# Far scores for two units at once from 64 contraction rows, in an attention, scan and feed-forward block on one core

## The reference

```
Q, K, V = x @ Wq.T, x @ Wk.T, x @ Wv.T          # 16 heads of 8
scores  = Q K^T * 8 ** -0.5
mask    = causal & ((col >= row - 31) | ((row - col) % 64 == 0))
attn    = softmax(where(mask, scores, -inf));    x += (attn @ V) @ Wo.T
h = s0 * [x, -x] @ sign(k0); relu * 2; s1 * h @ sign(k1); relu * 2; s2 * h @ sign(k2)   # feed-forward, added to x
state-space block: layernorm, conv over 4 steps, silu, dt = softplus(...),
  h = exp(dt * A) * h + dt * u * B ;  y = sum over 16 states of C * h     # 256 channels, a scan over time
feed-forward again
```

## Time and profile before

| | |
|---|---|
| median of 3 runs | 812.72 us |
| the profiled execution | 811.52 us, span of the core 809.7 us |
| PE busy | 721.4 us (89%) |
| DVE busy | 695.3 us (86%) |
| POOL busy | 664.2 us (82%) |
| ACT busy | 594.8 us (73%) |
| mean granted PE clock | 0.989 |

### The profile page before, as it was taken

One profiled execution on the slowest core, in us unless ns is written; L12 is line 12 of the kernel. 1 busy time (PEld: TensorE's weight loads), 2 busy tenths in 40 slices (PEclk: granted clock), 3 DMA queues, 4 the chain that ended last, 5 costly groups with the idle time before them and its releaser, 6 DMA issues. The chain is left out here.

```text
span 809.7 us, 22189 instructions
## 1 busy us (share of the span) xinstructions
PE 721.4 (89%) x7840; PEld 430.6 (53%) x7840; DVE 695.3 (86%) x1187; ACT 594.8 (73%) x1161; POOL 664.2 (82%) x824
## 2 busy tenths in 40 slices
PE   5999988998789999998999999899896889897887
PEld 3765655644455447545555456355452356453566
DVE  6977229999999989999889999999998989799983
ACT  5776698797788989887689978868667744764533
POOL 5143437998899989989999799899998999999961
PEclk9999999999999999999999999999999999998999
DMA  5000019888799668877777889889797899898950
GB/s 200 3 3 2 2 54 269 226 231 229 206 225 237 159 173 238 230 177 200 198 213 197 225 233 243 232 230 244 207 253 199 252 259 240 215 266 235 264 158 27
DMA packets 84177, 154.94 MB, mean 191 GB/s; under 512 B 9433, under 2 KB 10082, under 8 KB 84066
## 3 DMA queue, kind: packets, MB, share of 16 engines
q1 hardware_dynamic: 84066, 153.51, 71.4%
HBM read 142.46 MB, written 11.01 MB: 190 GB/s over the span
## 5 line engine op out<-in xcount | busy, mean ns | idle before, releaser
L1779 POOL TENSOR_TENSOR d<-d,cr 128x1024 f32<-128x1024 f32 x128 | 300.0, 2354 | 13.8 <-DVE d L1279 4.1
L1578 ACT ACTIVATE ps<-dt,An 128x512 f32<-128x512 f32 x256 | 173.7, 690 | 71.9 <-DVE d L1279 60.5
L1279 DVE TENSOR_TENSOR_SCAN d<-ps,hl,d 128x512 f32<-128x512 f32 x128 | 157.0, 1262 | 3.7 <-ACT ps L1578 3.3
L1279 DVE TENSOR_TENSOR_SCAN d<-ps,d 128x512 f32<-128x512 f32 x128 | 149.6, 1202 | 7.2 <-ACT ps L1578 6.5
L1267 DVE TENSOR_TENSOR d<-ps,d 128x512 f32<-128x512 f32 x184 | 118.5, 671 | 7.1 <-DMA d<-dud 7.1
L891 PE MATMUL ps<-h,w 128*128 128x512 f16 (+1 forms) x512 | 114.3, 373 | 3.5 <-DVE h L1224 2.8
L1766 POOL TENSOR_TENSOR d<-d,br 128x512 f32<-128x512 f32 x72 | 91.5, 1277 | 4.3 <-DMA d<-dud 4.3
L891 PEld LDWEIGHTS ps<-h,w 128*128 128x128 f16 x512 | 46.8, 98 | 70.9 <-DVE h L1224 12.8
L966 PE MATMUL ps<-d,cst 128*32 128x512 f32 x512 | 69.3, 614 | 10.6 <-POOL d L1779 6.4
L1434 ACT COPY pt<-ps 128x512 f32<-128x512 f32 x96 | 53.8, 589 | 13.9 <-PE ps L825 10.6
L825 PE MATMUL ps<-cst,sx 128*128 128x128 f32 x384 | 56.3, 281 | 8.0 <-ACT sx L1427 3.5
(11 more groups left out here) (182 smaller groups left out, 1457.1 us busy)
## 6 DMA issues: line engine op xcount, KB each, us to landing
dt<-dtd SPq DMA_DIRECT2D x256, 256.0 KB, 5.3
d<-dud SPq DMA_DIRECT2D x256, 256.0 KB, 4.8
dtd<-sR SPq DMA_DIRECT2D x16, 256.0 KB, 4.4
dud<-sE SPq DMA_DIRECT2D x16, 256.0 KB, 3.8
X<-in_x SPq DMA_DIRECT2D x8, 256.0 KB, 6.3
br<-bcd SPq DMA_DIRECT2D x8, 256.0 KB
cr<-bcd SPq DMA_DIRECT2D x8, 256.0 KB
out<-X SPq DMA_DIRECT2D x3, 512.0 KB, 5.8
```

Source lines behind the costliest of these rows:

```text
L1279: eng.tensor_tensor_scan(d, banks[u % NG][:, :], d, hl[:, r:r + 1] if m % 2 else 0.0, ALU.mult, ALU.add).then_inc(v_sc, 1)
L1578: eng.activation(banks[u % NG][:, :], DT[:, u % NT, :], ACT.Exp, scale=An[:, g:g + 1]).then_inc(s_da, 1)
L1779: eng.tensor_tensor(d, d, CR[m % 2][:, :].unsqueeze(1).to_broadcast((128, n, 512)), ALU.mult).then_inc(p_cm, n)
```

## The change

A far unit now has the eight heads of one half of the contraction rows and eight windows (before: all heads and four windows), and far units are made in pairs like near ones. The number of units is the same. Per far pair PE issues two mask products of 64 rows each (rows 0 to 63 and 64 to 127, in two banks) and 16 products of 64 contraction rows by 128 output rows by 64 columns. Per near pair it issues two such mask products and 8 products of 64 by 128 by 128 columns, in place of two full mask products and 16 of 64 by 64 by 128. `KD` has two copies instead of four, made by full 128 x 512 instructions scaled by a new constant `rmask` of ones and zeros per partition. POOL zeroes only the 64 leading columns of `KD`. The product with V keeps 16 products of 36 columns for a far unit. The second unit's flag (`t_sc`) comes with the pair's last product in both kinds.

All of `PLACES` is new. By its numbers, the median distance from the issue of a `du` row to its drive goes from 8351 to 9365, and from the issue of a `dt` row to its decay from 9727 to 10818. `WARM` goes from 28 entries with 152 products to 38 entries with 244 products; before the first scan there are five entries (18 products) where there were none.

```diff
-for _name, _n in (("ident", 128), ("qmask", 4), ("csel", 56), ("one8", 1)):
+for _name, _n in (("ident", 128), ("qmask", 4), ("csel", 56), ("one8", 1), ("rmask", 2)):
...
+    put("rmask", (p[:, None] // 32 % 2 == np.arange(2)[None, :]).astype(np.float32))
...
-UNITS = [(kind, g, kk) for kind, g in GROUPS for kk in range(2 if kind else 4)]
+UNITS = [(kind, g, kk, c) for kind, g in GROUPS for kk in range(1 if kind else 2) for c in range(2)]
...
 WARM = [
-    (125411, 2, 3), (127268, 2, 3), (173374, 5, 2), (180024, 6, 3), (216097, 5, 3), (460277, 5, 4), (465961, 2, 2), (505221, 7, 5),
...
+    (103369, 5, 4), (109970, 7, 5), (112856, 2, 3), (117704, 2, 2), (124035, 2, 4), (127533, 2, 7), (156348, 5, 3), (171612, 4, 3),
...
-        KD = sb("KD", [128, 4, PAD + T])
+        KD = sb("KD", [128, 2, PAD + T])
...
-        ZF = [sb(f"zf{i}", [128, 4, 4, 16]) for i in range(3)]
+        ZF = [sb(f"zf{i}", [128, 8, 2, 16]) for i in range(3)]
...
             def asc_t(b, u):
...
+                half = [slice(64 * c, 64 * c + 64) for c in range(2)]
+                two = []
+                for c in range(2):
+                    by = (s_exp, U + c + 1) if u + c in SHIFTED_T else (v_sub, shifted(b, u + c, "v") + 1)
+                    bank = bank_of["sc", b, u + c] = turn(by)
+                    if kind:
+                        mk = masks[half[c], 256:288].unsqueeze(1).to_broadcast((64, 16, 32))
...
+                    eng.matmul(bank[:, :], e4[half[c], :], mk, start=True, stop=False, skip_group_check=True)
+                    two.append(bank[:, :].rearrange("p (a w k) -> p a w k", a=2, w=nw))
...
-                    for k in range(4):
-                        m = 8 * g + 4 * kk + k
-                        lq = qm[:, 4 * kk + k, :, :].rearrange("p a n -> p (a n)")
-                        t = eng.matmul(bw[:, :, k, :].rearrange("p a (h x) -> p a h x", x=4), lq, Ks[:, :, :, 4 * m:4 * m + 4], start=False,
-                                       stop=(k == 3 and u not in SHIFTED_T), skip_group_check=True)
-                    t.then_inc(t_sc, 1)
-                    return
...
+                for k in range(nw):
+                    wi = nw * kk + k
+                    m = 8 * g + wi
                     for c in range(2):
...
+                        lq = qm[half[c], wi, :, :].rearrange("p a n -> p (a n)")
+                        dst = two[c][:, :, k, :]
+                        if kind:
+                            rk, dst = Ks[half[c], :, :, 4 * m:4 * m + 4], dst.rearrange("p a (h x) -> p a h x", x=4)
+                        else:
+                            at = 64 * (m % 16) + m // 16
+                            rk = KD[half[c], :, at:at + 127:2]
+                        t = eng.matmul(dst, lq, rk, start=False, stop=(k == nw - 1 and u + c not in SHIFTED_T), skip_group_check=True)
+                        if k == nw - 1:
                             t.then_inc(t_sc, 1)
...
-                eng.tensor_copy(e4[:, 32 * k:32 * k + 32], ident[:, 0:32]).then_inc(v_set, 2 if k == 3 else 1)
+                eng.tensor_tensor(e4[:, 32 * k:32 * k + 32], ident[:, 0:32], ident[:, 64:96], ALU.add).then_inc(v_set, 2 if k == 3 else 1)
...
-                    eng.wait_ge(p_set, 3)
                     eng.wait_ge(t_aqk, 1)
-                    for a in range(4):
-                        t = eng.tensor_copy(KD[32 * a:32 * a + 32, a, PAD:PAD + T:2], bank_of["aqk", b, 0, 1][32 * a:32 * a + 32, :])
+                    for a in range(2):
+                        t = eng.tensor_scalar(KD[:, a, PAD:PAD + T:2], bank_of["aqk", b, 0, 1][:, :], rmask[:, a:a + 1], None, ALU.mult)
...
-                for a in range(4):
-                    t = eng.copy(KD[32 * a:32 * a + 32, a, PAD + h:PAD + T:2], bank_of["aqk", b, h, 1][32 * a:32 * a + 32, :])
+                for a in range(2):
+                    t = eng.activation(KD[:, a, PAD + h:PAD + T:2], bank_of["aqk", b, h, 1][:, :], ACT.Identity, scale=rmask[:, a:a + 1])
...
-            eng.memset(KD[:, 0:3, :], 0.0).then_inc(p_set, 1)
+            eng.memset(KD[:, :, 0:PAD], 0.0).then_inc(p_set, 1)
...
-                eng.memset(KD[:, 3:4, :], 0.0).then_inc(p_set, 1)
```

More of the change, by code:

```diff
@@ L151 @@
     (UNITS_OF, 'aown_s apv_t asc_s asc_v atr_s atr_t'),
[L152 removed]
+    ([(b, u) for b, u in UNITS_OF if u % 2 == 0], 'asc_t'),
     ([(b, u) for b, u in UNITS_OF if u in SHIFTED_T], 'asb_t'),
@@ L748, in aval_t @@
                 t.then_inc(t_av, 1)
-            def scores(b, u, mk):
-                U = NU * b + u
-                bank = bank_of["sc", b, u] = turn((s_exp, U + 1) if u in SHIFTED_T else (v_sub, shifted(b, u, "v") + 1))
-                eng.matmul(bank[:, :], e4[:, :], mk, start=True, stop=False, skip_group_check=True)
-                return bank
             def asc_t(b, u):
-                kind, g, kk = UNITS[u]
+                kind, g, kk, _ = UNITS[u]
                 U, gi = NU * b + u, group_of(u)
+                nw = 8 if kind else 4
                 if U == 0:
                     eng.wait_ge(v_set, V_SEL)
-                if kind:
-                    bank = scores(b, u, masks[:, 256:288].unsqueeze(1).to_broadcast((128, 16, 32)))
-                else:
-                    kk, _ = near(u)
-                    if g == kk == 0:
-                        mk = masks[:, 0:256].unsqueeze(1).to_broadcast((128, 2, 256))
-                    else:
-                        mk = masks[:, 64:192].unsqueeze(1).to_broadcast((128, 4, 128))
-                    two = [scores(b, u + c, mk) for c in range(2)]
+                half = [slice(64 * c, 64 * c + 64) for c in range(2)]
[5 more added lines that the diff above has]
+                        mk = masks[half[c], 256:288].unsqueeze(1).to_broadcast((64, 16, 32))
+                    elif g == kk == 0:
+                        mk = masks[half[c], 0:256].unsqueeze(1).to_broadcast((64, 2, 256))
+                    else:
+                        mk = masks[half[c], 64:192].unsqueeze(1).to_broadcast((64, 4, 128))
+                    eng.matmul(bank[:, :], e4[half[c], :], mk, start=True, stop=False, skip_group_check=True)
+                    two.append(bank[:, :].rearrange("p (a w k) -> p a w k", a=2, w=nw))
                 if b == 0:
@@ L789, in asc_t @@
-                if g == 2:
-                    eng.wait_ge(p_kp, b + 1)
-                for k in range(4):
-                    m = 8 * g + 4 * kk + k
-                    at = 64 * (m % 16) + m // 16
-                    for c in range(2):
-                        r = slice(64 * c, 64 * c + 64)
-                        for j in range(2):
-                            o = slice(64 * j, 64 * j + 64)
-                            lq = qm[r, 4 * kk + k, 2 * j:2 * j + 2, :].rearrange("p a n -> p (a n)")
-                            dst = two[c][o, :].rearrange("p (a w k) -> p a w k", a=2, w=4)[:, :, k, :]
-                            t = eng.matmul(dst, lq, KD[r, 2 * c:2 * c + 2, at:at + 127:2], start=False,
-                                           stop=(k == 3 and u + c not in SHIFTED_T), skip_group_check=True)
-                        if k == 3:
+                Ks = KD[:, :, PAD:PAD + T].rearrange("p a (h x) -> p a h x", x=128)
@@ L1143, in asc_v @@
                 else:
-                    kk, c = near(u)
                     mm = MN[g % 2][:, 4 * kk:4 * kk + 4, 2 * c:2 * c + 2].rearrange("p w a -> p a w")
@@ L1361, in aqk_s @@
                         return
-                    eng.wait_ge(p_set, 3)
-                    for a in range(4):
-                        t = eng.copy(KD[32 * a:32 * a + 32, a, PAD + 1:PAD + T:2], bank_of["aqk", b, 1, 1][32 * a:32 * a + 32, :])
+                    for a in range(2):
+                        t = eng.activation(KD[:, a, PAD + 1:PAD + T:2], bank_of["aqk", b, 1, 1][:, :], ACT.Identity, scale=rmask[:, a:a + 1])
                     t.then_inc(s_aqk, 1)
```

276 lines of the change are left out of this document (136 added, 140 removed), and 318 rows, old and new, of tables (PLACES, WARM).

## The result

The changed kernel takes **823.21 us** (median of 10 runs, 817.05 to 831.07) against 812.98 us (808.44 to 818.95) for the kernel before on the same chip: a ratio of **1.0111, interval 1.0068 to 1.0154**. The ratio is that of the means without one execution of the changed kernel in which the chip was in a slower state (831.07 us), so it isn't the quotient of the two medians. By the medians the kernel is 10 us slower, by the ratio 9, where 6.5 us faster was forecast; the number lies in the range that was given, in the corner of rival B (822 us).

The account below looks back on a forecast made before the run. PE was taken to bound the kernel before 130 us, DVE and POOL together after; 811.5 less 2.3 (head), 2.2 (middle) and 2.0 (order) gave 805.0 us, as a median 806.2 against 812.7; range 796 to 824 us.

Parts of the forecast that it names:

- rival B: Far pair as one block on PE holds up work queued behind it: 1.0 us a pair, 822 us; chance 0.22.
- The near pairs: 32 near score pairs on PE: 1.61 us becomes 1.32, gain taken as 0.25 us a pair, 8.0 us in all.
- The two tiling changes: Switches of PE's array tiling, ahead of a near pair's masks and at its end, counted at 0.09 and 0.10 us.
- The far pairs: 16 far score pairs on PE: loads set the pace, 2.22 us becomes 2.19; gain taken as 0.05 us a pair.
- Rival C: Loads don't set the pace, far rounds on PE shrink to half of 0.111 us: 798 us; chance 0.12.
- Rival D: Weight loads of the two row halves on PE queue instead of running side by side: 844 us; chance 0.04.
- What passes to the end: Share of PE's saving that shortens the kernel: 2.3 us before 130 us, 2.2 us after it.
- the head's 2.3 us: Saving before 130 us, from 8 near and about 6 far pairs on PE, all taken to be on the path.
- B's signs: Wait of the far maximum well above 6.2 us, and over 653 us from first to last scan.
- The new order: New list asks for transfers about a ninth earlier relative to use: gain of 2 us, uncertainty of 10.
- Key copies: Fewer, fuller key copies on DVE and ACT (later ACT copies about 683 ns) and no POOL zeroing: hidden, 0 us.
- Warm products: 92 added on PE: between 24.7 us of delay and 8.9 us of clock given back; taken as 0.

Follow-up runs that it names:

- after_farhalf: The changed kernel with windows 4 to 7 of the far units given no products, only the mask: 808.88 us, ratio 0.9952 to the kernel before.
- after: The changed kernel itself, with new products, new list and 16 far pairs joined, against the kernel before: 823.21 us, ratio 1.0111.
- near_oldlist: The kernel before with only the near units changed; far units, key copies, order and warm products as before: 812.45 us, ratio 0.9981.

## Why the prediction was wrong, step by step

**The near pairs: right, and too careful.** 1.14 us mask to mask, 1.23 as the median of all, where 1.32 was forecast. The masks do stream together (0.22 us for two). The two tiling changes counted at 0.09 and 0.10 are hardly seen between neighbours of the same tiling, and the median has one of them. The gain a pair is 0.37 us by the medians (0.25 forecast).

**The far pairs: right in what paces them, mis-sized in the gain.** 1.96 us (forecast 2.19), so 0.26 us gained a pair where 0.05 was taken; the records take 1.73 us with both lanes together, where 1.8 to 1.9 was given. (Seven far pairs, not about six, stand ahead of the first scan.) Rival C would have been 0.9: a round of 64 columns takes 0.108 us, hardly less than a near round of 128 columns (8 rounds in 0.92 us) and than one record of 128 rows (0.111). The Trainium skill's "TensorEngine Tiling (Array Packing)", section "Theoretical Speedup", gives up to twice the speed for 64 contraction rows. The measured rounds show none of it for this shape. Rival D would have been 3.6: the loads of the two row halves run side by side.

**What passes to the end: mis-sized.** I took all of the head's 2.3 us and a third of the middle's. The near units alone give 1.4 us at the first scan and nothing between first and last scan. The third had no row behind it: "68 us idle on PE" says that PE's time has a lower price there, not which one. For near blocks in the old list it is about zero; for far blocks in the new list, from after_farhalf, about 0.9.

**The step that failed: the far pair as one block priced by its own length.** I counted 0.05 us gained a pair by comparing lengths from mask to mask, and held the rest as rival B with 0.22. The joining alone costs 0.0082 of the time, 0.8 us a pair in the head and 0.4 behind it. "Their maxima can be placed later" was the argument against B; the wait of the far maximum rose from 6.2 to 22.9 us instead, and the middle stretch from 652.9 to 660.5, which is what I had named as B's signs. B's price of 1.0 us a pair (16 us) was too high. That its total of 822 us fits is partly luck: it adds 16 us to gains of 6.5, of which the near units gave 1.5 and the order none that can be seen. I had the late end of the first unit and the blocked queue as one mechanism. The runs separate them: most of the price comes with the joining (1.0082), a smaller part, if any, with the late end (1.0103).

**The parts can be added up, which is not a proof.** Joining 1.0082, near units 0.9981, late first end 1.0103 − 1.0082 = 0.0021: together 1.0084. The three pairs that only after joins add about 3 x 0.4 us = 0.0015: 1.010, against 1.0111 (1.0068 to 1.0154) measured. But all these parts were measured in the old list, where adding doesn't work for the whole: there all new products give 1.0275. And the joining's price there holds a bank wait that the new list doesn't have. So the order, the added warm products and the head's clock may each cost or give several us that cancel. What is shown is that joining costs by itself, that the near products don't, and that in the new list the far blocks are on the path.

**The new order: no gain that can be seen.** I had taken 2 us because transfers are asked for earlier. But SyncE's issues still wait for the engines that free a tile. The queue's own waits in the changed kernel (total, times, longest):

```profile
SPq L685 <- PE ps L948: 114.0, 43, 11.6
SPq L676 <- ACT ps L1555: 101.9, 96, 4.7
```

Before they were 116.1 and 100.7 us, nearly the same. The waits for the transfers did fall, over the whole span from 7.1 to 5.0 us on DVE, from 4.3 to 1.0 on POOL and from 10.8 to 8.1 on ACT, and the time didn't fall with them. With old products the new list loses 10 us against the old one, with new ones it wins 13.

**Key copies: as forecast, nothing seen.** The 12 ACT copies take 8.0 us, 0.67 each (0.683 forecast).

**Warm products: open.** I took 0 for the 92 added. All 244 together are worth 2.4%; the 92 by themselves were not measured, and a number of that size did cost elsewhere (112 more on near_oldlist: 0.5%). The clock was not put at risk in the forecast, and it was: 10 us at half clock in the head. Its price could be read in one execution, but not in the medians.

**What stays open.** Why the new products lose 16 us in the old list. Three pairs there stand as single units on one row half, which costs each more PE time; the maxima wait 23.6 us; the clock falls to 0.947, and filling it made things worse. Which of these leads was not settled. Nor is it shown what the near units alone would give in the new list. Nor was it tried to take the far blocks' place earlier in the new list.

## What to carry to other kernels

A block's price is not its length. Ask for each block who waits for its result: of two kinds of score blocks, one gave back most of its microseconds (15.1 us of work, 13 of time, in the new list) and the other hardly any (8.7 us, 1.5, in the old list). Joining two blocks of a queue had a price of its own, with not a product changed; weigh it against the work that the joining saves, and try the part of the edit that joins nothing by itself. Here that, with the freed time filled, was 0.5% faster, where the whole change was 1.1% slower.

When a change brings products and a list of its own, run the four crossings. Here each half of the change looked good or bad by the other half it was paired with: the new products gained 0.9% in the new list and lost 1.9% in the old one.

## What the runs showed of the hardware

- Two 64-row products with 64 moving columns each, in the two row halves, take 0.108 us a round at full clock, where one record of 128 rows and 128 columns took 0.111 (a round is one record in each half). Halving both the rows and the moving columns gained nothing. The load kept its 128 columns, and near rounds with 128 moving columns took about the same (0.92 us for 8), so the load is the likely pace.
- Two 64-row masks of 512 columns in the two row halves take 0.22 us together, as one of 128 rows did.
- The granted clock fell to half for 10 us in the head of the changed kernel, behind the first 32-record far product and two short waits (0.75 and 0.78 us), and stayed full there with 4 warm products ahead of that block and 7 behind it.
- Warm products of 63.2 us on an engine that is 90% busy, all removed, made the kernel 2.4% slower and the mean clock 0.933 (0.979 with them).
- Two far units joined into one block, with the same products and both masks first, cost 0.82% for 13 pairs; in the head one block's second mask held PE for 1.32 us until an exponential on ACT had freed its bank.
